# An attention block on one core: the third tile's maxima in two parts, the first tile's operands from their own halves, the transpose one matmul later, two slots reordered, rows of x fetched singly

## The chip, the cores and the metric

The kernel runs on one core of a Trainium2 chip. The metric is the device time of one execution in microseconds (us).

## What is computed

For each of 16 batches, x is 512 channels by 1024 positions, in float32:

```python
qkv = jnp.einsum('bchw,oc->bohw', x, w_qkv)           # 8 heads of 64
sim = jnp.einsum('bhdi,bhdj->bhij', q * SCALE, k)      # 1024 x 1024 a head
attn = jax.nn.softmax(sim, axis=-1)
out = jnp.einsum('bhij,bhdj->bhid', attn, v)
y = jnp.einsum('bchw,oc->bohw', out, w_out) + b_out
y = y * jax.lax.rsqrt(mean over channels of y*y + SCALE) * rms_scale
return y + x
```

## The kernel before, in words

The engines are TensorE (PE), VectorE (DVE), ScalarE (ACT) and GpSimd (POOL); SyncE (SP) issues the DMAs. Every engine runs an instruction list written out by hand for all batches, and semaphores join them. Precision comes from splits: an operand is kept as a rounded high part and the rest as a low part (`x_hi`, `x_lo`), and a projection does three matmuls for one.

**Slots and places.** A batch is 8 slots, a slot being one pair of heads with one half (512) of the queries. A slot has 16 places t = 0 to 15. At the even ones stand the scores of a step of 128 keys: for each of the two heads e, a matmul of `q_hl` (line 611) and one of `q_hm` (line 613) that adds in the low parts and subtracts the row maximum. At t = 1, 5, 9, 13 stand the values of the two steps before (line 626), at t = 1 also the sums of the slot before (line 549), and then the maxima of one tile of 128 queries for the next slot: M0 at t = 1 to M3 at t = 13. At t = 3 and 7 stands a projection of 12 matmuls of 512 columns (K, line 465) or 24 of 256 (V, line 498), at t = 11 the output projection O0 and O1 (line 524, 12 matmuls), at t = 15 the next queries' projection Q (line 465, 12 matmuls). Slots 0 and 1 also hold the mean of squares R at t = 7. Slot 5 has nothing at t = 3.

**Maxima.** A tile's maxima need the scores of its 128 queries with all 1024 keys for both heads: four matmuls into the four `aux` banks of PSUM, head 0 in banks 0 and 1, head 1 in banks 2 and 3. DVE reduces head 0 in two parts. Item M (line 894) takes bank 0 and one column of bank 1 and leaves its result in that column, which frees bank 0; item N (line 900) then reduces bank 1 into `maxima`. Head 1 is one reduction of two banks (line 890). Where the two matmuls of a pair go to different halves of the array's rows, they run side by side. Mostly the pair is the two key halves of one head (line 589), which needs q and k in both halves of the partitions: ACT repeats them (lines 702, 704 and 713), at the place in `REPEAT_Q_AT`. In the slots of `EARLY_MAXIMA` (1, 2, 7) the first tile pairs the two heads instead, each from its own half (line 571), and needs no repeated operand.

**Transpose.** After M3 has been reduced, T (line 509) turns `maxima` into rows with one matmul of 128 columns, and DVE multiplies them by a mask into `q_hm` (line 906, twice); then the next slot's scores may start. T stands inside Q, after its first six matmuls. It waits until DVE has consumed N30 and M31.

**Banks.** `claim` makes PE wait until a bank's last item is consumed. O0 takes banks 0 and 1; O1 takes bank 2 for its first three matmuls and bank 3 for the next three. K, V and Q take bank 0, T and R bank 2.

**DVE's list in a slot.** Per place: the items, then the reciprocals of the sums (`INVERT_SUMS_AT`, line 946, two halves), the normalising (line 953), the scaling of y (`SCALE_AT`, line 959; slots 1 and 2 only), x's low parts (`SPLIT_LOW_AT`, line 305; slots 5 and 6). ACT turns the normalised output into `o_hi` at t = 7 (line 759), ahead of the exponentials of t = 8 (line 695), and the next scores into the same PSUM bank wait for those. POOL adds up the probabilities (lines 1043 and 1047), makes `o_lo`, and in slots 1 and 2 scales rows of y (line 1065) and adds x (line 1078, `RESIDUAL_AT`).

Of the kernel before, what the change touches and what calls it, by code (L numbers as in the profile page):

```python
# [13 lines left out]
P = 128  # L14
# [12 lines left out]
INVERT_SUMS_AT = ((2, 5), (2, 5), (2, 5), (2, 2), (2, 5), (5, 5), (2, 2), (2, 2))  # L27
# [4 lines left out]
REPEAT_Q_AT = (0, 3, 3, 0, 0, 0, 0, 0)  # L32
# [3 lines left out]
EARLY_MAXIMA = (1, 2, 7)  # L36

# [12 lines left out]
SCALE_BY_ACT_AT = ((0, 3), (1, 3))  # L52
SCALE_AT = ({1: (1, 2), 2: (1, 3), 3: (1, 6)}, {2: (2, 2), 3: (2, 3)})
# [4 lines left out]
SPLIT_LOW_AT = ((5, 1), (5, 0), (5, 3), (5, 2), (6, 5), (6, 6), (6, 9), (6, 12))  # L58
SPLIT_BY_GPSIMD = (1, 3, 5, 7)


def items_at(slot, t, first, last):
# [4 lines left out]
    out = []  # L67
    if t % 4 == 1 and following:
        out.append((f"M{t // 4}0", 0))
        out.append((f"N{t // 4}0", 1))  # L70
        out.append((f"M{t // 4}1", 2))
    if t in (3, 7):
# [15 lines left out]
    if t == 15:  # L88
# [4 lines left out]
        if slot == 6 and projected:  # L93
# [5 lines left out]
             (7, "M10", 0), (7, "N10", 1), (7, "M11", 2), (7, "V2", 0), (7, "V3", 2), (7, "M20", 0), (7, "N20", 1), (7, "M21", 2),  # L99
# [21 lines left out]
def attention_kernel(nc, x, wqkv, wout, bias, scale, consts, out):  # L121
# [27 lines left out]
    with ctx:  # L149
# [91 lines left out]
        out_stored = sem("out_stored")  # L241
# [59 lines left out]
        def split_x(eng, c, n):  # L301
# [5 lines left out]
                              ).then_inc(x_split[c % 2], 1)  # L307
# [31 lines left out]
        def _(sp):  # L339
# [14 lines left out]
            for c in range(XS, 2 * KT):  # L354
                sp.wait_ge(x_split[c % 2], (c - XS) // 2 + 1)
                load_x(0, c)
# [21 lines left out]
            def finish_half(b, half, body_after=None):  # L378

                done = b * 2 + half  # L380
                cols = slice(half * HALF, (half + 1) * HALF)
                if half == 1 or body_after is None:
                    sp.wait_ge(out_stored, 16 * MT * done)
                for m in range(MT):
                    sp.dma_start(resid[:, m, :], x_v[b, m, :, cols]).then_inc(resid_loaded[m], 16)
                for m in range(MT):
                    sp.wait_ge(resid_added, 4 * done + m + 1)
                    sp.dma_start(out_v[b, m, :, cols], resid[:, m, :]).then_inc(out_stored, 16)

            def one(body):  # L390
# [5 lines left out]
                if not body.first:  # L396
                    finish_half(b - 1, 0, body)
                body.full(sp, 1, "Q")
                load_w(3)
                if not body.first:  # L400
                    finish_half(b - 1, 1, body)
                if not body.last:
# [8 lines left out]
                    if not body.first:  # L411

                        sp.wait_ge(out_stored, 16 * MT * 2 * b)
                    load_x(b + 1, XS - 1)
                    for c in range(XS, 2 * KT):
                        sp.wait_ge(x_split[c % 2], KT * (b + 1) + (c - XS) // 2 + 1)
# [5 lines left out]
            finish_half(B - 1, 0)  # L422
            finish_half(B - 1, 1)
            sp.wait_ge(out_stored, 16 * MT * 2 * B)
# [3 lines left out]
        def _(pe):  # L428
# [27 lines left out]
            def wait_x(body, half):  # L456

                for by in x_split:
                    pe.wait_ge(by, KT * (body.b + 1) + KT // 2 * (half + 1))

            def project(out_ap, w, cols, xcols, ks=range(KT)):

                for k in ks:
                    for n, (wp, xp) in enumerate(((0, x_hi), (1, x_hi), (0, x_lo))):
                        last = pe.matmul(out_ap, w[:, wp, k, cols], xp[:, k, xcols],  # L465
# [3 lines left out]
            def item(body, slot, name, ks=range(KT)):  # L469
                if name == "Q":  # L470
                    wait_w(body, (slot + SLOT_QUERIES) % SLOTS // 2, slot >= SLOTS - SLOT_QUERIES)
                    k = body.at(slot, name)[0] if ks[0] else claim(body, slot, name)
                    half = slot % 2
                    last = project(bank(k), w_ring[:, RING_OF[(slot + SLOT_QUERIES) % SLOTS // 2]], slice(0, P),
                                   slice(half * HALF, (half + 1) * HALF), ks)
                    if ks[-1] == KT - 1:
                        last.then_inc(aux_full[k], 1)
# [8 lines left out]
                elif name[0] == "V":  # L486
# [4 lines left out]
                    for i in range(2):  # L491
                        jt = 2 * int(name[1]) + i
                        n = 0
                        for c in range(KT):
                            if name == "V0" and slot == 5 and i == 0:
                                pe.wait_ge(x_split[c % 2], KT * (body.b + 1) + c // 2 + 1)
# [671 lines left out]
```

## Time and profile before

| | us |
|---|---|
| median of 3 runs | 4129.59 (4129.58 to 4131.71) |
| the profiled execution | 4120.75 |
| its span | 4119.0 |
| before the first scores | 56.1 |
| PE busy | 4022.6 |
| POOL busy | 2939.3 |
| DVE busy | 2885.2 |
| ACT busy | 2315.2 |

The span is from the first instruction of the program to the last. Matmuls are pipelined, so PE's busy share doesn't tell how well it is used; the distance from one matmul's start to the next one's does. A batch takes some 252 us, a slot 29.1 to 34.0.

### The profile page before, as it was taken

Reading aid. Unit: us, or ns where it says so; the run is one execution under the profiler, and the core shown is the slowest. Engines: PE = TensorE matmul, PEld = TensorE weight load, DVE = VectorE, ACT = ScalarE, POOL = GpSimd, SP = SyncE. Lnnn points to the kernel's source line nnn. Section 1 sums busy time; section 2 is a strip of 40 time slices with the busy share of each in tenths; the row PEclk is TensorE's granted clock in tenths of the full one; section 3 lists DMA queues with packets and bytes.
Section 4 is the critical chain, followed back from the end, with each engine's and each line's share of the span. In section 5 each row is a group of like instructions: output and inputs, shape, how many; then the busy total and the mean of one; then the engine's idle time right before and its main releaser. Section 6 shows DMA issues by size and latency. Waiting matters only on the chain.

```text
span 4119.0 us, 53911 instructions
## 1 busy us (share of the span) xinstructions
PE 4022.6 (98%) x18624; PEld 2413.1 (59%) x18624; DVE 2885.2 (70%) x3151; ACT 2315.2 (56%) x4044; POOL 2939.3 (71%) x2279
## 2 busy tenths in 40 slices
PE   7999999999999999999999999999999999999996
PEld 5555565665656555566655655556556565665652
DVE  5667776777766777676776766777667776777765
ACT  3556555565655656555565655655556565565653
POOL 4668676786776868767686776867768676686866
PEclk9999999999999999999999999999999999999998
DMA  3111111111111111112011110110111111111100
GB/s 144 41 37 57 52 42 62 52 52 41 63 51 42 52 42 67 47 42 72 32 62 52 37 67 31 62 52 37 67 52 42 52 44 62 49 52 42 65 19 31
DMA packets 71278, 212.25 MB, mean 52 GB/s; under 512 B 8152, under 2 KB 8280, under 8 KB 58208
## 3 DMA queue, kind: packets, MB, share of 16 engines
q1 hardware_dynamic: 71008, 208.80, 14.2%
q8 instruction: 151, 2.47, 0.3%
q14 instruction: 119, 0.97, 0.1%
HBM read 168.92 MB, written 39.85 MB: 51 GB/s over the span
## 4 chain that ended last, share of the span: by engine, by line
PE 77%; issue 7%; ACT 7%; DVE 5%; POOL 4%; DMA 0%; ACTq 0%; POOLq 0%; SPq 0%; DVEq 0%
PE pv L626 16%; PE aux L465 15%; PE score L611 11%; PE score L613 9%; PE aux L498 8%; PE aux L524 8%; PE aux L589 6%; ACT probs L695 3%; POOL prob_sum L1047 2%; ACT q_hm L704 1%; ACT q_hl L702 1%; DVE inv_sum L946 1%; ACT q_hl L720 1%; DVE maxima L890 1%; PE aux L509 1%
## 5 line engine op out<-in xcount | busy, mean ns | idle before, releaser
L1047 POOL TENSOR_TENSOR prob_sum<-prob_sum,probs 128x512 f32<-128x512 f32 x1536 | 1957.7, 1302 | 395.9 <-ACT probs L695 395.1
L695 ACT ACTIVATE probs<-score 128x512 f32<-128x512 f32 x2048 | 1110.5, 595 | 896.9 <-PE score L613 885.5
L626 PE MATMUL pv<-probs,v_sb 128*64 128x512 f32 x4096 | 993.3, 606 | 0.0
L894 DVE TENSOR_REDUCE aux<-aux 128x1 f32<-128x513 f32 x512 | 358.1, 699 | 904.8 <-PE aux L589 833.4
L611 PE MATMUL score<-q_hl,k_hh 128*128 128x512 f32 x2048 | 868.9, 424 | 13.7 <-ACT probs L695 11.9
L613 PE MATMUL score<-q_hm,k_l 72*128 72x512 f32 x2048 | 815.4, 398 | 0.0
L1043 POOL TENSOR_TENSOR prob_sum<-probs 128x512 f32<-128x512 f32 x256 | 352.4, 1398 | 461.4 <-ACT probs L695 461.4
L465 PE MATMUL aux<-x_hi,w_ring 128*128 128x512 f32 x2048 | 649.8, 398 | 15.6 <-DVE x_lo L305 11.1
L890 DVE TENSOR_REDUCE maxima<-aux 128x1 fp32r<-128x1024 f32 x512 | 621.4, 1214 | 0.0
L611 PEld LDWEIGHTS score<-q_hl,k_hh 128*128 128x128 f32 x2048 | 387.1, 189 | 278.8 <-issue 163.7
L626 PEld LDWEIGHTS pv<-probs,v_sb 128*64 128x64 f32 x4096 | 248.2, 136 | 483.0 <-issue 435.7
L946 DVE RECIPROCAL inv_sum<-inv_sum 128x256 f32<-128x256 f32 x256 | 438.7, 1735 | 9.5 <-ACT inv_sum L753 6.0
L465 PEld LDWEIGHTS aux<-x_hi,w_ring 128*128 128x128 f32 x2048 | 376.2, 190 | 101.1 <-issue 12.7
L613 PEld LDWEIGHTS score<-q_hm,k_l 72*128 72x128 f32 x2048 | 389.2, 190 | 59.3
L465 PE MATMUL aux<-x_lo,w_ring 128*128 128x512 f32 x1024 | 402.6, 393 | 0.0
L498 PE MATMUL aux<-w_ring,x_hi 128*128 128x256 f32 x2048 | 375.8, 284 | 1.7 <-DVE aux L894 1.7
L900 DVE TENSOR_REDUCE maxima<-aux 128x1 fp32r<-128x512 f32 x512 | 353.7, 691 | 17.6
L589 PEld LDWEIGHTS aux<-k_hh,q_hm 64*128 64x128 f32 x922 | 135.9, 185 | 391.2 <-issue 211.1
L589 PE MATMUL aux<-k_hh,q_hm 64*128 64x512 f32 x922 | 336.7, 445 | 10.5 <-DVE k_l L883 3.9
L589 PE MATMUL aux<-k_hh,q_hl 64*128 64x512 f32 x922 | 336.4, 444 | 0.0
L498 PEld LDWEIGHTS aux<-w_ring,x_hi 128*128 128x128 f32 x2048 | 326.3, 192 | 16.2 <-DVE aux L894 8.0
L498 PE MATMUL aux<-w_ring,x_lo 128*128 128x256 f32 x1024 | 290.6, 284 | 0.0
(84 smaller groups left out, 4898.6 us busy)
## 6 DMA issues: line engine op xcount, KB each, us to landing
w_ring<-w_split SPq DMA_DIRECT2D x93, 1024.0 KB, 4.8
x_stage<-x SPq DMA_DIRECT2D x128, 256.0 KB, 4.7
resid<-x SPq DMA_DIRECT2D x128, 256.0 KB, 5.8
out<-resid SPq DMA_DIRECT2D x128, 256.0 KB, 2.0
w_split<-w_ring SPq DMA_DIRECT2D x3, 1024.0 KB, 11.9
w_split<-y_sb SPq DMA_DIRECT2D x3, 1024.0 KB, 3.8
y_sb<-wqkv SPq DMA_DIRECT2D x4, 512.0 KB, 8.0
probs<-wqkv SPq DMA_DIRECT2D x2, 512.0 KB, 7.2
```

The source lines that it names most:

```text
L465: last = pe.matmul(out_ap, w[:, wp, k, cols], xp[:, k, xcols], start=(k == 0 and n == 0), stop=(k == KT - 1 and n == 2))
L498: last = pe.matmul(bank(k)[:, i * WCOLS:(i + 1) * WCOLS], xp[:, c, jt * P:(jt + 1) * P], w[:, wp, c, :], start=(n == 0), stop=(n == 3 * KT ...
L589: last = pe.matmul(bank(k + h), q_hi_at(nhalf, e, h, it), k_hh[rows, npair % 2, e, h * HALF:(h + 1) * HALF], start=True, stop=True)
L611: pe.matmul(score[e][:], k_hh[:, pair % 2, e, keys], q_hl[:, half, e, :], start=True, stop=False)
L613: pe.matmul(score[e][:], k_l1[0:D + 2 * IT, pair % 2, e, keys], q_hm[0:D + 2 * IT, half, e, :], start=False, stop=True).then_inc(score_rea ...
L626: pe.matmul(pv[half][e * D:(e + 1) * D, :], v_sb[:, pair // 2, j, (pair % 2) * P + e * D:(pair % 2) * P + (e + 1) * D], probs[:, j % 4, e, ...
L695: act.activation(probs[:, j % 4, e, :], score[e][:], ACT.Exp, scale=SOFT).then_inc(prob_ready, 1)
L890: dve.tensor_reduce(maxima[:, n:n + 1], bank(k, 2), AX_X, ALU.max).then_inc(aux_free[k], 1)
L894: dve.tensor_reduce(aux[:, first:first + 1], aux[:, k * HALF:first + 1], AX_X, ALU.max).then_inc(aux_free[k], 1)
L900: dve.tensor_reduce(maxima[:, n:n + 1], bank(k), AX_X, ALU.max).then_inc(aux_free[k], 1)
L946: dve.reciprocal(inv_sum[:, cols], inv_sum[:, cols]).then_inc(inv_ready, 1)
L1047: pool.tensor_tensor(prob_sum[:, e, :], prob_sum[:, e, :], probs[:, j % 4, e, :], ALU.add).then_inc(prob_added, 1)
```

## The change

The constants: slot 2 inverts its second half of the sums at t = 6 (before at 5), and scales rows 2 and 3 of y at t = 5 and 10 (before at 2 and 3). Slot 5 inverts at t = 2 and 5 (before both at 5), repeats the queries at t = 2 (before at 0), and DVE makes the low parts of pieces 0 and 1 of the next x at t = 0 (before pieces 0 and 2 at t = 1 and 3); POOL now has pieces 2, 3, 5, 7. ACT scales POOL's rows of y at t = 6 (before 3). The first tile's maxima use own halves in every slot. The third tile's head 1 is reduced in two parts like head 0. T follows Q's seventh matmul. The first score matmul of a slot goes ahead of the wait for the mask. SP has a semaphore for each of the four rows of the output; it loads a row of x for the second half as soon as that row of the first half is stored, and does so ahead of the weights of chunk 3.

```diff
-INVERT_SUMS_AT = ((2, 5), (2, 5), (2, 5), (2, 2), (2, 5), (5, 5), (2, 2), (2, 2))
+INVERT_SUMS_AT = ((2, 5), (2, 5), (2, 6), (2, 2), (2, 5), (2, 5), (2, 2), (2, 2))
-REPEAT_Q_AT = (0, 3, 3, 0, 0, 0, 0, 0)
+REPEAT_Q_AT = (0, 3, 3, 0, 0, 2, 0, 0)
-EARLY_MAXIMA = (1, 2, 7)
+SPLIT_SECOND = (2,)
+TURN_OF_MAXIMA = 7
-SCALE_BY_ACT_AT = ((0, 3), (1, 3))
-SCALE_AT = ({1: (1, 2), 2: (1, 3), 3: (1, 6)}, {2: (2, 2), 3: (2, 3)})
+SCALE_BY_ACT_AT = ((0, 6), (1, 6))
+SCALE_AT = ({1: (1, 2), 2: (1, 3), 3: (1, 6)}, {2: (2, 5), 3: (2, 10)})
-SPLIT_LOW_AT = ((5, 1), (5, 0), (5, 3), (5, 2), (6, 5), (6, 6), (6, 9), (6, 12))
-SPLIT_BY_GPSIMD = (1, 3, 5, 7)
+SPLIT_LOW_AT = ((5, 0), (5, 0), (5, 2), (5, 2), (6, 5), (6, 6), (6, 9), (6, 12))
+SPLIT_BY = ((0, 1, 4, 6), (2, 3, 5, 7))
...
-            def finish_half(b, half, body_after=None):
...
+            def load_resid(b, half):
                 for m in range(MT):
+                    if half == 1:
+                        sp.wait_ge(out_stored[m], 16 * (2 * b + 1))
+                    sp.dma_start(resid[:, m, :], x_v[b, m, :, half * HALF:(half + 1) * HALF]
+                                 ).then_inc(resid_loaded[m], 16)
...
+                    load_resid(b - 1, 0)
+                    store_half(b - 1, 0)
+                    load_resid(b - 1, 1)
                 body.full(sp, 1, "Q")
                 load_w(3)
...
+                        if turn and 3 * k + n == TURN_OF_MAXIMA:
+                            item(turn[0], turn[1], "T")
...
-                if it == 0 and slot in EARLY_MAXIMA or body.plan is pro:
+                if it == 0 or body.plan is pro:
+                    split = (True, it in SPLIT_SECOND)
...
-                if it == (1 if slot in EARLY_MAXIMA else 0):
+                if it == 1:
                     pe.wait_ge(q_repeated, 2 * (body.b * SLOTS + slot + 2))
...
+                    keys = slice(j * P, (j + 1) * P)
+                    pe.matmul(score[e][:], k_hh[:, pair % 2, e, keys], q_hl[:, half, e, :],
+                              start=True, stop=False)
                     if j == 0 and e == 0:
                         pe.wait_ge(mask_ready, body.b * SLOTS + slot + 1)
...
-                    keys = slice(j * P, (j + 1) * P)
-                    pe.matmul(score[e][:], k_hh[:, pair % 2, e, keys], q_hl[:, half, e, :],
-                              start=True, stop=False)
...
-                    if name[2] == "1":
+                    if name[2] == "1" and int(name[1]) not in SPLIT_SECOND:
```

## Rows read from the trace of the kernel before

**Rows 1.** The page: span, busy time by engine, TensorE's granted clock in 40 slices.
```profile
span 4119.0 us, 53911 instructions
...
PE 4022.6 (98%) x18624; PEld 2413.1 (59%) x18624; DVE 2885.2 (70%) x3151; ACT 2315.2 (56%) x4044; POOL 2939.3 (71%) x2279
...
PEclk9999999999999999999999999999999999999998
```

**Rows 2.** Waits: engine and line, released by; us in total, times, longest.
```profile
PEld aux L509 <- DVE maxima L890: 64.9, 128, 3.3
...
PEld aux L524 <- DVE maxima L890: 46.3, 111, 0.6
```

**Rows 3.** Groups of DVE by shape: count, busy us, mean ns, idle before.
```profile
L894 DVE TENSOR_REDUCE aux<-aux 128x1 f32<-128x513 f32 x512 | 358.1, 699 | 904.8 <-PE aux L589 833.4 <-PE aux L571 71.0
...
L900 DVE TENSOR_REDUCE maxima<-aux 128x1 fp32r<-128x512 f32 x512 | 353.7, 691 | 17.6
...
L959 DVE SCALAR_TENSOR_TENSOR y_sb<-y_sb,scale_sb,rms_a 128x512 f32<-128x512 f32 x83 | 100.8, 1235 | 1.2 <-ACT rms_a L793 0.7
```

**Rows 4.** Timeline, slot 0 of batch 4, M3 to the next scores.
```profile
1088.01 0.70 DVE L894 TENSOR_REDUCE aux<-aux 128x1 f32<-128x513 f32 x1 [0.45 <-PE aux L589]
...
1089.35 1.21 DVE L890 TENSOR_REDUCE maxima<-aux 128x1 fp32r<-128x1024 f32 x1
...
1090.02 0.19 PEld L465 LDWEIGHTS aux<-x_lo,w_ring 128*128 128x128 f32 x1
1090.24 0.40 PE L465 MATMUL aux<-x_lo,w_ring 128*128 128x512 f32 x1
...
1090.68 0.19 PEld L509 LDWEIGHTS aux<-neg_ident,maxima 128*128 128x128 f32 x1 [0.47 <-DVE maxima L890]
1090.71 0.30 PE L509 MATMUL aux<-neg_ident,maxima 128*128 128x128 f32 x1
...
1091.04 1.28 DVE L906 TENSOR_TENSOR q_hm<-aux,tile_mask 8x512 fp32r<-8x512 f32 x2 [0.48 <-PE aux L509]
...
1092.26 0.39 PE L611 MATMUL score<-q_hl,k_hh 128*128 128x512 f32 x1
```

**Rows 5.** Timeline, the same slot, M2 and the output projection.
```profile
1079.74 0.50 PE L589 MATMUL aux<-k_hh,q_hm 64*128 64x512 f32 x1
...
1081.72 1.21 DVE L890 TENSOR_REDUCE maxima<-aux 128x1 fp32r<-128x1024 f32 x1
...
1082.61 0.40 PE L524 MATMUL aux<-o_lo,wo_hi 128*128 128x512 f32 x1
...
1082.98 0.50 PE L524 MATMUL aux<-o_hi,wo_hi 128*128 128x512 f32 x1
...
1083.32 0.39 PE L524 MATMUL aux<-o_hi,wo_lo 128*128 128x512 f32 x1
```

**Rows 6.** Timeline, sums and M0: slot 0 (first two), slot 1.
```profile
1063.48 1.03 PE L549 MATMUL pv<-prob_sum,ones_d 128*64 128x512 f32 x4
...
1064.56 0.18 PEld L589 LDWEIGHTS aux<-k_hh,q_hm 64*128 64x128 f32 x1 [0.94 <-ACT q_hm L704]
...
1095.06 1.03 PE L549 MATMUL pv<-prob_sum,ones_d 128*64 128x512 f32 x4
...
1096.01 0.18 PEld L571 LDWEIGHTS aux<-k_hh,q_hm 64*128 64x128 f32 x1 [0.81 <-issue]
```

**Rows 7.** Timeline, slot 2 of batch 3 (starts at 872.42), M1 to the fifth scores.
```profile
883.11 1.60 DVE L959 SCALAR_TENSOR_TENSOR y_sb<-y_sb,scale_sb,rms_a 128x512 f32<-128x512 f32 x1
...
884.18 0.50 PE L611 MATMUL score<-q_hl,k_hh 128*128 128x512 f32 x1
...
888.39 0.39 PE L611 MATMUL score<-q_hl,k_hh 128*128 128x512 f32 x1
```

**Rows 8.** Timeline, slot 5 of batch 3 (starts at 966.35), reciprocals to the sixth scores.
```profile
978.56 3.35 DVE L946 RECIPROCAL inv_sum<-inv_sum 128x256 f32<-128x256 f32 x2
...
983.84 0.50 PE L611 MATMUL score<-q_hl,k_hh 128*128 128x512 f32 x1 [0.24 <-ACT probs L695]
```

More of the change, by code:

```diff
@@ L71, in items_at @@
         out.append((f"M{t // 4}1", 2))
+        if t // 4 in SPLIT_SECOND:
+            out.append((f"N{t // 4}1", 3))
     if t in (3, 7):
@@ L240, in attention_kernel @@
         resid_loaded = [sem(f"resid_loaded{i}") for i in range(MT)]
-        out_stored = sem("out_stored")
+        out_stored = [sem(f"out_stored{i}") for i in range(MT)]
         x_loaded = [sem(f"x_loaded{i}") for i in range(XS)]
@@ L421, in _ @@
             run_bodies(sp, one)
-            finish_half(B - 1, 0)
-            finish_half(B - 1, 1)
-            sp.wait_ge(out_stored, 16 * MT * 2 * B)
+            wait_stored(2 * (B - 1))
+            for half in range(2):
+                load_resid(B - 1, half)
+                store_half(B - 1, half)
+            wait_stored(2 * B)
         @block.tensor
@@ L456, in wait_x, with project @@
             def wait_x(body, half):
[L458 to L463, printed above, removed]
+                for c in (max(c for c in by if c < KT * (half + 1)) for by in SPLIT_BY):
+                    wait_piece(pe, c, body.b + 1)
+            def project(out_ap, w, cols, xcols, turn=None):
+                for k in range(KT):
                     for n, (wp, xp) in enumerate(((0, x_hi), (1, x_hi), (0, x_lo))):
+                        if turn and 3 * k + n == TURN_OF_MAXIMA:
+                            item(turn[0], turn[1], "T")
                         last = pe.matmul(out_ap, w[:, wp, k, cols], xp[:, k, xcols],
@@ L467, in project, with item @@
                 return last
-            def item(body, slot, name, ks=range(KT)):
+            def item(body, slot, name, turn=None):
                 if name == "Q":
                     wait_w(body, (slot + SLOT_QUERIES) % SLOTS // 2, slot >= SLOTS - SLOT_QUERIES)
-                    k = body.at(slot, name)[0] if ks[0] else claim(body, slot, name)
+                    k = claim(body, slot, name)
                     half = slot % 2
[L474 to L477, printed above, removed]
+                    project(bank(k), w_ring[:, RING_OF[(slot + SLOT_QUERIES) % SLOTS // 2]], slice(0, P),
+                            slice(half * HALF, (half + 1) * HALF), turn).then_inc(aux_full[k], 1)
                 elif name[0] == "K":
@@ L563, in maxima_of_tile @@
                 npair, nhalf = divmod(nslot, 2)
-                if it == 0 and slot in EARLY_MAXIMA or body.plan is pro:
-                    ks = [claim(body, slot, f"M{it}0"), claim(body, slot, f"M{it}1", two=True)]
-                    claim(body, slot, f"N{it}0")
+                if it == 0 or body.plan is pro:
+                    split = (True, it in SPLIT_SECOND)
+                    ks = [claim(body, slot, f"M{it}{e}", two=not split[e]) for e in range(2)]
+                    for e in range(2):
+                        if split[e]:
+                            claim(body, slot, f"N{it}{e}")
                     for h in range(2):
@@ L583, in maxima_of_tile @@
                 for e in range(2):
-                    k = claim(body, slot, f"M{it}{e}", two=e == 1)
+                    split = e == 0 or it in SPLIT_SECOND
+                    k = claim(body, slot, f"M{it}{e}", two=not split)
                     for h in range(2):
-                        if h == 1 and e == 0:
-                            claim(body, slot, f"N{it}0")
+                        if h == 1 and split:
+                            claim(body, slot, f"N{it}{e}")
                         rows = slice(h * D, (h + 1) * D)
@@ L653, in one @@
                         elif "Q" in names:
[L654 to L656 removed]
+                            item(body, slot, "Q", (body, slot))
                             for name in names:
@@ L990, in one @@
                         if (slot, t) in SPLIT_LOW_AT and not body.last:
-                            if SPLIT_LOW_AT.index((slot, t)) not in SPLIT_BY_GPSIMD:
-                                split_x(dve, SPLIT_LOW_AT.index((slot, t)), body.b + 1)
+                            for c in SPLIT_BY[0]:
+                                if (slot, t) == SPLIT_LOW_AT[c]:
+                                    split_x(dve, c, body.b + 1)
             dve.memset(ones_d[:], 1.0).then_inc(const_set, 1)
@@ L999, in _ @@
             split_w(0, 0)
-            for c in range(0, 2 * KT, 2):
+            for c in SPLIT_BY[0]:
                 split_x(dve, c, 0)
-                if c == 2:
+                if c == 1:
                     split_w(1, VA)
@@ L1101, in one @@
                             split_squares_low(2 * (body.b - 1) + slot)
-            for c in range(1, 2 * KT, 2):
+            for c in SPLIT_BY[1]:
                 split_x(pool, c, 0)
```

48 lines of the change are left out of this document (24 added, 24 removed).

## The prediction

> **What bounds the kernel now.** I read the page first: PE is busy nearly the whole span, its granted clock at the full level (2.4 GHz) after the prologue, and no other engine is busy above 71% [rows 1]. So time is gained only where the step from one matmul's start to the next is longer than it need be. The usual step for 512 columns is 0.23 us. Next the waits, for those of PE that come back in every slot: the transpose T waits for DVE's last maximum 128 times, the second output projection 111 times [rows 2]. Then the timeline around each, for what the wait costs PE; and last the starts of all score matmuls (line 611), sixteen a slot, which show in which slots a step between scores is longer than in others with the same work. The reader is to see that all losses are short, on PE, and repeat in each batch.
>
> **T one matmul later.** Q's sixth matmul starts at 1090.24. DVE's reduction ends at 1089.35 + 1.21 = 1090.56, T's weights load at 1090.68 and T runs at 1090.71 [rows 4]: 0.47 after the sixth matmul, where 0.23 is usual. The loss is 0.23 to 0.24, in all slots alike (the mean step over the 128 T is 0.468). After the change the seventh matmul fills it: it starts at 1090.47, T's turn is at 1090.70, and DVE allows it at 1090.71. One matmul fits as exactly as the trace can tell. Gain 0.233 in each slot that has Q beside T: 8 in each of 15 batches and 6 in the last, 126 x 0.233 = 29.4 us. What this uncovers is the mask: T now has 5 matmuls behind it, so the scores start 1.33 after T and not 1.55 (1092.26 - 1090.71). DVE's first mask multiply ends 0.33 + 0.64 = about 1.0 after T (half of the 1.28) and the second at 1.61 [rows 4]. With the first score matmul ahead of the wait, what needs the masks starts at 1.56 (head 0) and 2.03 (head 1), its weights 0.23 before. With the 0.12 that T's load took after DVE's end both are in time, the second by under 0.1. Without this reorder the second would be late by 0.1 to 0.2; I count the reorder itself at nothing.
>
> The Trainium skill ("TensorE: Matmul & The Clock Gate", The mechanism) says that a weight load overlaps matmuls in flight only when its row group differs. By that T's own load of 0.19 would be exposed wherever T stands, and the move would gain about 0.05 a slot. The trace disagrees: the 128-row load at 1090.02 runs inside the matmuls of 128 rows before it [rows 4].
>
> **Third tile in two parts.** M2 starts at 1079.74; head 1's reduction runs from 1081.72 to 1082.93. Output matmul 6 starts at 1082.61, matmul 7, which needs bank 2, at 1082.98 and matmul 8 at 1083.32: steps of 0.37 and 0.34 for 0.23 each [rows 5], a loss of 0.25. In two parts bank 2 comes free after 0.70 [rows 3], at 1082.42, before its turn; bank 3 after another 0.03 + 0.69, at 1083.14, and is needed by a load at 1083.3. Gain 0.25 x 111 = 27.8 us. The 111 are the waits [rows 2]; in slot 5 PE comes late for another reason and doesn't wait. The cost is on DVE: 0.70 + 0.03 + 0.69 for 1.21, 0.21 a slot, 27 us in all. It lies in DVE's idle time: before M3's first reduction DVE has been idle for 0.45 in slot 0 [rows 4], the least of all slots by the same view, of which about 0.15 goes because PE reaches M3 sooner. If the cover were gone, M3's reductions and with them T would be late by as much as is lacking.
>
> **First tile from own halves.** In slot 0 M0 starts 1.08 after the sums, when ACT's repeat of q ends; in slot 1, which has the form already, 0.95 [rows 6]. Gain 0.125 in slots 0, 3, 4, 5, 6, so 80 x 0.125 = 10.0 us. Head 0's banks are then full 0.2 later, which slots 1, 2 and 7 bear without loss. M1 waits for the repeats instead, and they end 4 us earlier.
>
> **Slot 2.** DVE's scaling of row 3 (1.60 us) ends only at 884.71, so M1's reductions come late and K1, which needs bank 0, too: the fourth scores start at 884.18, the fifth at 888.39, 4.21 after, where slot 0 without R has 3.80 [rows 7]. Over the 15 batches that scale y this step is 4.13 to 4.21 eight times, 4.44 six times, 6.05 once; the step before is 3.56 to 4.47. Together these lose 13.5 us. After the change nothing stands before M1 but half a reciprocal, but behind it come the scaling of row 2, the other reciprocal (1.74), the normalising (0.69) and then K1's two subtractions (1.38), and M2 needs K1's bank. From M1's start: reductions done at 3.2, scaling 4.4, reciprocal 6.1, normalised 6.8, K1's bank free 8.2; M2's turn comes at 3.56 + 3.80 = 7.36. It waits 0.86, 12.9 us over 15 batches. Net gain 0.6. The scaling is the uncertain term: it took 1.60 here with POOL at work and 1.24 on the mean [rows 3, 7], with 0.65 and 1.81 as its ends by the same view. I take the mean, since POOL adds probabilities without a pause at that point and DVE would come in the middle of one addition. The ends give slot 2 a net of +9 and -8 us. The Trainium skill ("SBUF — State Buffer", Who interferes with whom) says that a DVE instruction with two SBUF inputs and a reading GpSimd instruction exclude each other for a whole instruction, whoever is first. The two durations of one form agree.
>
> Row 3's scaling moves to t = 10, and POOL waits for it inside its step 4, with three steps of additions queued behind. I put its sum of x and row 3 at 25.6 from the slot's start. ACT's copy of O1's last row waits for that; the exponentials behind it end at 26.9, and the eighth scores need them at 27.3. POOL's last addition ends some 1.1 before the sums need it. Nothing, with 0.4 to spare.
>
> **Slot 5.** The normalising waits for two reciprocals in a row (3.35), ACT holds the exponentials behind `o_hi`, and the sixth scores start only at 983.84 [rows 8], 3.87 after the fifth for 3.56: 0.31. One half moves to t = 2, and the low parts of x to t = 0, where DVE waits for M0 anyway (two at 0.65 with POOL idle, done at 4.5, M0's reductions at 4.58). Also 0.06 where ACT's repeat leaves the second exponentials free. 0.37 x 15, and 1.8 in the last batch, where slot 5 has no V: 7.4 us. If the two low parts took 1.8 each, M0's reductions would be late by 2.3, and M1's banks with them: 2 us a batch, 30 in all.
>
> **The rest at nothing.** ACT's two scalings at t = 6 lie in its idle time, and leave slot 1's repeat of q earlier, at most 0.08 a batch, 1 us in all. The single fetches and the four semaphores act on SP; the loads ahead of chunk 3's weights wait for stores that land some 5 us before the end of slot 1, and those weights are first needed two slots later. What is queued behind SP's waits has that room. POOL's and DVE's pieces of x in the prologue: within 0.3 us either way.
>
> **Sum.** 29.4 + 27.8 + 10.0 + 0.6 + 7.4 = 75.2 us. The profiled execution took 4120.75 and becomes 4045.5; the median of the runs is 8.8 above it, and becomes 4054.4. A difference of 0.2%, 8 us, is about what a measurement of this kernel can tell from none.
>
> **The rivals.**
>
> T's pause stays, as a cost of its own (an exposed load, or DVE just late again): 29.4 x 0.8 less, 4078. For it: the fit has no margin. Against: T's load started 0.12 after the reduction's end in 127 of 128, so it waited. Chance 0.08.
>
> DVE becomes the wait: its extra 0.21 a slot reaches PE at O1's second bank or at M3. 4054 + 111 x 0.2 = 4077 if in full. For: margins of 0.15 and 0.3. Chance 0.12.
>
> Slot 2 or 5 worse than counted: the long ends, 8 + 15 or so, 4077. Chance 0.12.
>
> Slot 2 without its new wait (the scaling finds POOL's gap): 4054 - 9 = 4045. Chance 0.08.
>
> Slower: in slot 2 POOL, held at row 3, finishes the additions late; PE's sums, and ACT's exponentials of the reused probability buffers, wait for them. It decides from (75 + 8) / 15 = 5.5 us a batch. By my schedule POOL has 1.1 to spare and is idle twice before, so it would have to be wrong by 6.6: 4140. Chance 0.03.
>
> **How the numbers follow.** The forecast, 4054, has 0.57 with its own range of 4046 to 4064. The cases near 4077 have 0.32 in all, the one at 4045 0.08, the slower one 0.03. The range 4039 to 4083 leaves out less than 0.2. Faster by over 0.2% 0.94, within 0.2% 0.03, slower 0.03.
>
> **What would show it.** T's step 0.24 in place of 0.47 and no idle time of the weight load before it; output matmuls 7 and 8 at 0.23; M0 0.95 after the sums in all slots; one new wait, of M2 in slot 2 for line 883, near 0.9; slot 5 at 28.4 us from 29.1. The prediction is wrong if T's weights still wait over 0.2 for DVE, if line 509 or 524 keeps its wait, or if POOL's list becomes continuous through slots 2 and 3.

## The result, and the profile after

The changed kernel takes 4029.51 us (median of 4, 4027.74 to 4029.71), the kernel before 4129.59 (4 runs, 4121.6 to 4131.71). The ratio is 0.976, 95% interval 0.9743 to 0.9777: faster by 2.4%. The forecast was 4054 with a range of 4039 to 4083, so the sign was right and the gain was too small, outside the range. The profiled execution took 4027.74 (4120.75 before), its span fell by 93.0.

The page of the changed kernel (beside [rows 1]):

```profile
span 4026.0 us, 53767 instructions
...
PE 3951.3 (98%) x18624; PEld 2427.4 (60%) x18624; DVE 2890.0 (72%) x3279; ACT 2320.3 (58%) x4044; POOL 2919.8 (73%) x2279
...
PEclk9999999999999999999999999999999999999997
...
L916 DVE TENSOR_REDUCE aux<-aux 128x1 f32<-128x513 f32 x640 | 446.7, 698 | 849.7 <-PE aux L611 636.3
```

PE is as full as before and does the same matmuls in 71 us less busy time. DVE has 128 reductions more, PE 208 and SP 32 waits more that are instructions of their own, and yet the program has 144 instructions fewer: 512 waits of DVE are gone. They are what the prediction missed, as experiment 9 shows.

Its waits, beside [rows 2] (line 527 is T, 611 the maxima of M1 to M3, 903 DVE's subtraction for K):

```profile
PEld aux L527 <- DVE maxima L910: 26.8, 128, 3.2
...
PE aux L611 <- DVE k_l L903: 10.0, 15, 0.7
```

T's wait fell from 64.9 to 26.8, 0.21 on the mean, and did not go away. The 46.3 of the output projection have no row any more. The new wait is M2's in slot 2, 15 times, as forecast.

The timeline at the end of slot 0 of batch 4, beside [rows 4]: M3, DVE's reductions, Q's seventh matmul, T, the masks, the next scores.

```profile
1062.91 0.50 PE L611 MATMUL aux<-k_hh,q_hm 64*128 64x512 f32 x1
...
1063.48 0.70 DVE L916 TENSOR_REDUCE aux<-aux 128x1 f32<-128x513 f32 x1 [0.38 <-PE aux L611]
...
1064.82 1.21 DVE L910 TENSOR_REDUCE maxima<-aux 128x1 fp32r<-128x1024 f32 x1
...
1066.01 0.40 PE L485 MATMUL aux<-x_hi,w_ring 128*128 128x512 f32 x1
1066.15 0.19 PEld L527 LDWEIGHTS aux<-neg_ident,maxima 128*128 128x128 f32 x1 [0.17 <-DVE maxima L910]
1066.25 0.23 PE L527 MATMUL aux<-neg_ident,maxima 128*128 128x128 f32 x1
1066.31 0.45 PE L485 MATMUL aux<-x_hi,w_ring 128*128 128x512 f32 x1
...
1066.51 1.28 DVE L928 TENSOR_TENSOR q_hm<-aux,tile_mask 8x512 fp32r<-8x512 f32 x2 [0.48 <-PE aux L527]
...
1067.52 0.40 PE L626 MATMUL score<-q_hl,k_hh 128*128 128x512 f32 x1
```

T stands 0.24 after the matmul ahead of it, as forecast. But two more things changed. DVE starts 0.57 after M3's first matmul, where it was 0.64 (M3 of before started at 1087.37, the reduction at 1088.01 [rows 4]). And the matmul behind T follows it by 0.06, where it was 0.13.

The same slot, third tile and output projection, beside [rows 5]: head 1's two reductions and matmuls 6 to 8.

```profile
1057.44 0.69 DVE L916 TENSOR_REDUCE aux<-aux 128x1 f32<-128x513 f32 x1
...
1058.16 0.69 DVE L922 TENSOR_REDUCE maxima<-aux 128x1 fp32r<-128x512 f32 x1
...
1058.40 0.39 PE L542 MATMUL aux<-o_lo,wo_hi 128*128 128x512 f32 x1
...
1058.63 0.40 PE L542 MATMUL aux<-o_hi,wo_hi 128*128 128x512 f32 x1
...
1058.87 0.39 PE L542 MATMUL aux<-o_hi,wo_lo 128*128 128x512 f32 x1
```

Bank 2 is free at 1058.13, 0.5 ahead of its turn; all steps are 0.23 to 0.24.

Sums and M0 in slot 0, beside [rows 6]:

```profile
1039.38 1.03 PE L567 MATMUL pv<-prob_sum,ones_d 128*64 128x512 f32 x4
...
1040.34 0.18 PEld L592 LDWEIGHTS aux<-k_hh,q_hm 64*128 64x128 f32 x1 [0.81 <-issue]
```

0.96 after the sums for 1.08, with no releaser on ACT. Slot 2 of batch 3 (starts at 852.09), beside [rows 7]:

```profile
866.33 1.23 DVE L981 SCALAR_TENSOR_TENSOR y_sb<-y_sb,scale_sb,rms_a 128x512 f32<-128x512 f32 x1
867.48 1.74 DVE L968 RECIPROCAL inv_sum<-inv_sum 128x256 f32<-128x256 f32 x1
867.67 0.39 PE L626 MATMUL score<-q_hl,k_hh 128*128 128x512 f32 x1
...
869.86 1.38 DVE L903 TENSOR_TENSOR k_l<-aux,k_hh 64x512 fp32r<-64x512 f32 x2
...
871.29 0.49 PE L611 MATMUL aux<-k_hh,q_hm 64*128 64x512 f32 x1 [0.65 <-DVE k_l L903]
...
871.95 0.50 PE L626 MATMUL score<-q_hl,k_hh 128*128 128x512 f32 x1
```

The scaling takes 1.23 (I had taken 1.24). M2 waits for K1's bank, and the sixth scores come 4.28 after the fifth for 3.56. The two steps ahead of that are at 3.56 and 3.82 to 3.84 in all 15 batches that scale y. Slot 5 of batch 3, beside [rows 8], fifth and sixth scores:

```profile
957.79 0.40 PE L626 MATMUL score<-q_hl,k_hh 128*128 128x512 f32 x1
...
961.35 0.51 PE L626 MATMUL score<-q_hl,k_hh 128*128 128x512 f32 x1
```

3.56 for 3.87, and no wait for ACT. The starts of all score matmuls in the two traces, step by step, give the sum, in us:

| | forecast | measured |
|---|---|---|
| T and Q (last step of a slot) | 29.4 | 38.7 |
| output projection | 27.8 | 31.0 |
| first tile | 10.0 | 9.9 |
| slot 2, net | 0.6 | 2.0 |
| slot 5 | 7.4 | 7.3 |
| slot 1 | up to 1 | 1.0 |
| start of the program and first slot | 0 | 3.9 |
| rest | 0 | -0.8 |
| span | 75.2 | 93.0 |

So the profiled execution is 17.8 faster than forecast (4045.5), 9.3 of it in T's term. Another 7.0 come from the step to the median: I carried over the 8.8 by which the profiled execution of before lies under its median; after the change it is 1.8.

### The profile page after: what moved, and what is told of

It reads as the page before. It is cut to its first block, busy times and chain, and to the rows that moved or that the text cites. A ratio compares the mean times of both kernels' runs of the same rounds, so it can differ in the third digit from the quotient of the medians.

```text
span 4026.0 us, 53767 instructions
## 1 busy us (share of the span) xinstructions
PE 3951.3 (98%) x18624; PEld 2427.4 (60%) x18624; DVE 2890.0 (72%) x3279; ACT 2320.3 (58%) x4044; POOL 2919.8 (73%) x2279
## 4 chain that ended last, share of the span: by engine, by line
PE 94%; DVE 3%; issue 2%; POOL 1%; ACT 0%; DMA 0%; POOLq 0%; SPq 0%; ACTq 0%; DVEq 0%
PE pv L648 23%; PE aux L485 17%; PE score L626 14%; PE score L635 11%; PE aux L516 9%; PE aux L542 9%; PE aux L611 6%; PE pv L567 3%; PE aux L592 2%; DVE inv_sum L968 1%; DVE maxima L910 1%; DVE k_l L903 1%; DVE y_sb L981 0%; DVE aux L916 0%; ACT probs L715 0%
## 5 line engine op out<-in xcount | busy, mean ns | idle before, releaser
L916 DVE TENSOR_REDUCE aux<-aux 128x1 f32<-128x513 f32 x640 | 446.7, 698 | 849.7 <-PE aux L611 636.3
L1066 POOL TENSOR_TENSOR prob_sum<-probs 128x512 f32<-128x512 f32 x256 | 338.3, 1343 | 505.9 <-ACT probs L715 505.9
L910 DVE TENSOR_REDUCE maxima<-aux 128x1 fp32r<-128x1024 f32 x384 | 465.9, 1213 | 0.0
L922 DVE TENSOR_REDUCE maxima<-aux 128x1 fp32r<-128x512 f32 x640 | 442.4, 691 | 22.0
L485 PEld LDWEIGHTS aux<-x_hi,w_ring 128*128 128x128 f32 x2048 | 386.8, 189 | 95.6 <-issue 12.4
L516 PEld LDWEIGHTS aux<-w_ring,x_hi 128*128 128x128 f32 x2048 | 328.4, 192 | 13.9 <-DVE aux L916 2.4
L611 PEld LDWEIGHTS aux<-k_hh,q_hm 64*128 64x128 f32 x762 | 112.1, 184 | 320.2 <-issue 244.2
L611 PE MATMUL aux<-k_hh,q_hm 64*128 64x512 f32 x762 | 278.0, 444 | 10.0 <-DVE k_l L903 10.0
L611 PE MATMUL aux<-k_hh,q_hl 64*128 64x512 f32 x762 | 277.7, 444 | 0.0
```

The source lines that it names most:

```text
L516: last = pe.matmul(bank(k)[:, i * WCOLS:(i + 1) * WCOLS], xp[:, c, jt * P:(jt + 1) * P], w[:, wp, c, :], start=(n == 0), stop=(n == 3 * KT ...
L611: last = pe.matmul(bank(k + h), q_hi_at(nhalf, e, h, it), k_hh[rows, npair % 2, e, h * HALF:(h + 1) * HALF], start=True, stop=True)
L910: dve.tensor_reduce(maxima[:, n:n + 1], bank(k, 2), AX_X, ALU.max).then_inc(aux_free[k], 1)
L916: dve.tensor_reduce(aux[:, first:first + 1], aux[:, k * HALF:first + 1], AX_X, ALU.max).then_inc(aux_free[k], 1)
L922: dve.tensor_reduce(maxima[:, n:n + 1], bank(k), AX_X, ALU.max).then_inc(aux_free[k], 1)
```

## The experiments

Kernels are changed from the changed kernel unless it says otherwise. "Over" and "under" are differences of medians against 4029.51. The kernel before, timed beside each group again, had medians of 4123.7 (0 to 3), 4127.19 (4 to 7), 4127.62 (9 to 12) and 4128.01 (13, 14). The numbers go from 7 to 9. The changed kernel itself was timed only in the four runs above, and the kernel before moves by up to 6 us from group to group (4129.59 in the first). A difference of a few microseconds therefore rests on the steps in the traces, which are given beside it. Experiments 13 and 14 ran on a second chip; the kernel before took the same there within 0.4 us.

**0. The kernel before again**, unchanged.

> The kernel before, unchanged, timed again. The four timed runs of it lie at 4121.6 and near 4130, those of the changed kernel within 2 us. Theory A (slot 2's race for SBUF between VectorE and GpSimd comes out otherwise from run to run): times scatter by up to 10 us and slot 2's steps before the fourth and fifth scores lose between 10 and 25 us in all, 13.5 in the first profile. Theory B (the spread was of the chip that day): times within 2 us of each other, slot 2 loses 13 to 14.

4124.54 (11 runs, 4117.73 to 4127.64) beside 4123.7 (15 runs, 4118.07 to 4129.03); ratio 1.0002 (0.9993 to 1.001). These 11 executions spread over 10 us, those of the changed kernel over 2, but the latter are four, all at a mean granted clock of 0.993, where these have 0.991 to 0.993. Slot 2's two steps lose as much in this trace as in the first one, within 1 us, though in other batches. So the traces do not show that the race between VectorE and GpSimd (Theory A) makes the scatter.

**1. T after six matmuls.**

```diff
-TURN_OF_MAXIMA = 7
+TURN_OF_MAXIMA = 6
```

> The changed kernel with the transpose back behind the sixth matmul. Prediction's size (the wait for VectorE alone, 0.233 a slot): 29 us slower, 4059. Theory now (the wait also costs the weight load behind the transpose, 0.07, since it can't be fetched ahead): 0.30 a slot, 38 us slower, 4068. Rival (the extra 0.07 comes from the score matmul ahead of the mask wait): 29 us slower, and the step from the transpose to the next matmul stays 0.066.

4057.62, 28.1 over; ratio 0.9842 (0.9829 to 0.9855). The end of slot 0 of batch 4:

```profile
1075.00 0.40 PE L485 MATMUL aux<-x_lo,w_ring 128*128 128x512 f32 x1
1075.37 0.19 PEld L527 LDWEIGHTS aux<-neg_ident,maxima 128*128 128x128 f32 x1 [0.40 <-DVE maxima L910]
1075.40 0.30 PE L527 MATMUL aux<-neg_ident,maxima 128*128 128x128 f32 x1
1075.53 0.68 PE L485 MATMUL aux<-x_hi,w_ring 128*128 128x512 f32 x2
```

With T in its old turn the two steps around it are 0.40 and 0.13. They were 0.47 and 0.13 before, and are 0.24 and 0.06 in the changed kernel. The turn is worth 0.23 a slot, as forecast; the 38 us of "Theory now" were wrong, and so was the rival's step of 0.066, which is 0.13. The turn does not explain the drop from 0.47 to 0.40: something else brings DVE 0.07 forward in every slot.

**2. Third tile whole.**

```diff
-SPLIT_SECOND = (2,)
+SPLIT_SECOND = ()
```

In the prologue, item N21 goes too.

> The changed kernel with head 1 of the third tile reduced in one instruction of two banks. Prediction: 28 us slower, 4057. From the trace after: 0.25 to 0.30 in seven slots and slot 5 too, now that nothing else holds it back there: 31 to 35 us slower, 4061 to 4064. Rival (VectorE's 27 us less work gives something back): less than 25 us slower.

4056.59, 27.1 over; ratio 0.984 (0.9826 to 0.9853). The step of the output projection is 0.18 to 0.24 longer in every slot. The prediction's 28 was right, my 31 to 35 from the trace after was not.

**3. First tile from repeated operands** in slots 0, 3, 4 and 6.

```diff
+EARLY_MAXIMA = (1, 2, 5, 7)
...
-                if it == 0 or body.plan is pro:
+                if it == 0 and slot in EARLY_MAXIMA or body.plan is pro:
...
-                if it == 1:
+                if it == (1 if slot in EARLY_MAXIMA else 0):
```

> The changed kernel with slots 0, 3, 4 and 6 pairing the key halves again for the first tile and waiting for the repeated queries. Prediction: 0.125 in 4 slots of 16 batches, 8 us slower, 4037.5. Rival (the repeats are no longer late since the scalar engine starts sooner): no difference.

4039.09, 9.6 over; ratio 0.9797 (0.9782 to 0.9812). By the steps it is 0.125 in each of the four slots, 8 us in all; the profiled execution's first scores also came 2.7 later.

**4. Slot 2 in the old order.**

```diff
-INVERT_SUMS_AT = (..., (2, 6), ...)
+INVERT_SUMS_AT = (..., (2, 5), ...)
-SCALE_AT = (..., {2: (2, 5), 3: (2, 10)})
+SCALE_AT = (..., {2: (2, 2), 3: (2, 3)})
```

> The changed kernel with slot 2's reciprocal and two scalings at their old places. Prediction: 0.6 us slower. Theory now: the old order loses 13.5 us or more in 15 batches and varies from run to run, the new one 11.0 and doesn't: 3 to 12 us slower, 4033 to 4041, with a scatter over 3 us. Rival (the gain over the median came from elsewhere): within 2 us, no scatter.

4022.69, 6.8 *under* the changed kernel; ratio 0.9748 (0.9734 to 0.9761). In batches 1 to 14 (of 0 to 15) the steps are 6.2 us shorter. M2's wait is gone, and the third and fourth steps between scores (to the fourth and fifth scores) are 3.56 and 4.06 to 4.15 in all 15 batches, where the kernel before, with the same order, has 3.56 to 4.47 and 4.13 to 6.05. So the old order's erratic loss vanished without its being reordered, and the new order is a loss.

**5. The mask's wait first**, ahead of the first score matmul.

```diff
-                    keys = slice(j * P, (j + 1) * P)
-                    pe.matmul(score[e][:], k_hh[:, pair % 2, e, keys], q_hl[:, half, e, :],
-                              start=True, stop=False)
                     if j == 0 and e == 0:
                         pe.wait_ge(mask_ready, body.b * SLOTS + slot + 1)
...
                     elif j == 0:
                         body.consumed(pe, slot - 1, "T")
+                    keys = slice(j * P, (j + 1) * P)
+                    pe.matmul(score[e][:], k_hh[:, pair % 2, e, keys], q_hl[:, half, e, :],
+                              start=True, stop=False)
```

> The changed kernel with the wait for the mask back ahead of the first score matmul. Prediction: the second mask is late by 0.1 to 0.2 a slot less the slack of 0.2 that a weight load has, so 0 to 13 us slower, 4030 to 4043. Rival (the reorder is worth its own matmul, 0.23 a slot): 29 us slower, 4059.

4033.1, 3.6 over; ratio 0.9771 (0.9757 to 0.9784). The first step of a slot is 0.02 longer, 2.2 us in batches 1 to 14. I had put the lateness that the reorder covers at 0.1 to 0.2. The edit also gives PE 254 more waits that are instructions of their own (54021 instructions for 53767), so it stays open whether the 0.02 is a late mask or these.

**6. Slot 5 as before.**

```diff
-INVERT_SUMS_AT = (..., (2, 5), (2, 2), (2, 2))
-REPEAT_Q_AT = (0, 3, 3, 0, 0, 2, 0, 0)
-SPLIT_LOW_AT = ((5, 0), (5, 0), (5, 2), (5, 2), ...)
-SPLIT_BY = ((0, 1, 4, 6), (2, 3, 5, 7))
+INVERT_SUMS_AT = (..., (5, 5), (2, 2), (2, 2))
+REPEAT_Q_AT = (0, 3, 3, 0, 0, 0, 0, 0)
+SPLIT_LOW_AT = ((5, 1), (5, 0), (5, 3), (5, 2), ...)
+SPLIT_BY = ((0, 2, 4, 6), (1, 3, 5, 7))
...
-                if c == 1:
+                if c == 2:
                     split_w(1, VA)
```

> The changed kernel with slot 5's list (reciprocals, repeat of the queries, pieces of x and who makes their low parts) as before, in the prologue too. Prediction: 7.4 us slower. If the 2.2 us that the first scores came earlier are of the order of the pieces of x, 9.6 us slower, 4039, and the first scores at 56.1. Rival (the 2.2 us are of the third tile's split or of chance): 7.4 us slower, first scores at 54.

4040.27, 10.8 over; ratio 0.9788 (0.9775 to 0.9801). Slot 5 is 0.46 longer (0.18 in its second step, 0.31 in its fifth, 0.03 less in its sixth), the last batch 4.4 longer, the first scores 1.8 later. That last part is no proof for the order of the pieces of x: the two traces of the kernel before, with one and the same order, have their first scores at 56.1 and 53.5.

**7. T after eight matmuls.** `TURN_OF_MAXIMA = 8`.

> The changed kernel with the transpose one matmul later still. Theory (seven matmuls fill the wait exactly): nothing to gain, and the masks come later by one matmul: the second is late by 0.1 to 0.2, so 0 to 20 us slower. Rival (a wait is left behind seven, 26.8 us of idle weight loads): up to 8 us faster.

4027.06, 2.4 under; ratio 0.9756 (0.9743 to 0.9769). The last step is 3.944 for 3.954, and all steps of batches 1 to 14 together are 2.3 us shorter: T's turn had almost no more to give, and nothing was lost by later masks.

**9. The second wait put back.** The missed edit is in DVE's part: before, a two-part reduction waited for its own bank *and* for the next one; after, for the next one alone, since the later matmul implies the earlier.

```diff
                     else:
+                        k = body.full(dve, slot, name)
                         body.full(dve, slot, "N" + name[1:])
-                        k, _ = body.at(slot, name)
```

> The changed kernel with VectorE's list for a tile's first reduction as before: a wait for the bank of the first part and then one for the second, where the change has only the latter. Theory (the second wait costs an instruction of its own, 0.067 between the maxima's matmuls and their first reduction, and this reaches the transpose in every slot): 0.067 x 126 = 8.4 us slower, 4038. Rival (the 0.067 came from the first tile's form or the fetches): no difference.

4039.22, 9.7 over; ratio 0.9787 (0.9774 to 0.9801). Its page's first line, and the end of slot 0 of batch 4:

```profile
span 4038.1 us, 54407 instructions
```

```profile
1069.17 0.50 PE L611 MATMUL aux<-k_hh,q_hm 64*128 64x512 f32 x1
...
1069.81 0.70 DVE L916 TENSOR_REDUCE aux<-aux 128x1 f32<-128x513 f32 x1 [0.45 <-PE aux L611]
...
1072.27 0.40 PE L485 MATMUL aux<-x_hi,w_ring 128*128 128x512 f32 x1
1072.48 0.19 PEld L527 LDWEIGHTS aux<-neg_ident,maxima 128*128 128x128 f32 x1 [0.24 <-DVE maxima L910]
1072.51 0.30 PE L527 MATMUL aux<-neg_ident,maxima 128*128 128x128 f32 x1
1072.64 0.45 PE L485 MATMUL aux<-x_hi,w_ring 128*128 128x512 f32 x1
```

640 instructions more than the changed kernel, one for each of DVE's 640 two-part reductions (x640 on the page). The instructions by source line show what they are in the kernel before, where there were 512:

```profile
L288 DVEq EVENT_SEMAPHORE  x512: 21/21/21, 25.5 to 4045.8; - x171
```

A second wait is an instruction of its own on DVE's queue. It takes 0.021, and with it the reduction starts 0.64 after M3's first matmul and not 0.57. In the kernel before, that instruction stands at 1087.94, 0.57 after M3's first matmul, which is when the reduction itself starts in the changed kernel; the reduction follows 0.04 after its end. T's step is 0.24 and the one behind it 0.13: these are the steps that I had costed. The step behind T falls to 0.06 only when DVE is early enough for T's weights to load ahead of T's turn, which takes the turn and the one wait together.

**10 and 14. The kernel before with one wait**, the same edit alone, twice.

```diff
-                    k = body.full(dve, slot, name)
+                    k, _ = body.at(slot, name)
                     if name[2] == "1":
+                        body.full(dve, slot, name)
```

> The kernel before with this one wait taken out of VectorE's list and nothing else. Theory: the transpose comes 0.067 earlier in every slot (8.4 us), and in slot 2 VectorE's scaling is ready 0.067 earlier and goes ahead of GpSimd's addition every time, which takes away some 8 of slot 2's 13.5 us: 12 to 17 us faster than before, near 4110. Rival (no race, only the wait): 8 us faster.

> The kernel before with DVE's second wait taken away, run a second time. Its first median was 30.7 below the kernel before (4096.95), its profiled span only 18.5 below. If the profiled execution was simply an outlier (its last batch 3.1 longer, prologue 1.4 longer), the median is again 4095 to 4099 and this profile's span is near 4096 to 4101, 20 us less over batches 1 to 14. If the first median was the chance, it is 4100 to 4108 now.

4096.95 and 4097.05 beside 4127.62 and 4128.01: ratios 0.9927 (0.9913 to 0.994) and 0.9924 (0.9911 to 0.9936), 31 us by one wait, where I had expected 12 to 17. In batches 1 to 14 both traces show some 22 us less: 0.07 in every last step (8.5), 0.07 in the step of the output projection (7), and 6 to 7 us in two steps of slot 2, far more than 0.07 a batch. Both profiled executions were the longest of their five (4102.25 and 4100.06) and that of before was short (4120.75), so the profiles show less than the medians. The medians of executions with the same recorded clock, within a group, lie 29 to 32 apart, so the clock doesn't explain the rest.

What happened in slot 2 is the scaling of row 2 by DVE. In the 19 batches of the two traces in which GpSimd was not held up by a late row of x, it took 0.65 every time.

**11. The rows of x behind the weights** (on top of 4): the four loads of the second half after chunk 3's weights and after all four stores, as before the change.

```diff
                     store_half(b - 1, 0)
-                    load_resid(b - 1, 1)
                 body.full(sp, 1, "Q")
                 load_w(3)
                 if not body.first:
+                    wait_stored(2 * b - 1)
+                    load_resid(b - 1, 1)
```

> The changed kernel with slot 2's list as before, and the second half's rows of x loaded behind chunk 3's weights and after all four stores, as before. Theory (the single fetches matter where slot 2 scales early: in 5 of 15 batches of the kernel before, GpSimd's first sum of x waited for its row): 1 to 4 us slower than with the early loads, 4024 to 4027, with rows late in some batches. Rival (the loads are hidden either way): 4022.7, no row late.

4020.79, 1.9 under experiment 4; ratio 0.9742 (0.9729 to 0.9756). GpSimd's first sum of x starts at 6.17 from slot 2's start in all batches of experiment 4, at 6.29 to 6.66 in four of these, and slot 2's third and fourth steps lose 1.5 us more in 14 batches, in the range that I had expected, but the median does not show it. The single fetches bring nothing that the times show.

**12. Best version**: experiment 4, T after eight, and only row 3's scaling at its new place.

```diff
-TURN_OF_MAXIMA = 7
+TURN_OF_MAXIMA = 8
-INVERT_SUMS_AT = (..., (2, 6), ...)
+INVERT_SUMS_AT = (..., (2, 5), ...)
-SCALE_AT = (..., {2: (2, 5), 3: (2, 10)})
+SCALE_AT = (..., {2: (2, 2), 3: (2, 10)})
```

> The changed kernel with the reciprocals of slot 2 as before, row 2's scaling at place 2 as before, row 3's at place 10 as changed, and the transpose after eight matmuls. From slot 2 as before 4022.7; less 2 for the transpose; less 0.27 x 15 = 4 if K1 no longer waits: 4017. Rival (GpSimd, held at row 3, is late for the sums): slower than 4022.

4015.62 (4012.12 to 4016.4), 13.9 under; ratio 0.9728 (0.9715 to 0.9742). Slot 2's third to sixth steps are 3.56, 3.83, 3.56 and 3.82: no wait is left in them.

**13. Two waits in the old slot 2**: experiment 4 with the edit of 9.

> The changed kernel with slot 2 in its old order and early fetches of x (measured at 4022.7), with the second wait put back ahead of DVE's two-part reductions. It tells what the second wait does in slot 2. If the two waits only delay each reduction by 0.067, the cost is that of the same edit in the changed kernel, 9.7: 4032, slot 2's fourth and fifth steps stay at 3.56 and 4.1 in all batches, and DVE's scaling of row 2 takes 0.65 there. If the delay makes DVE lose the race with GpSimd for that scaling (it won by 0.03 with one wait), the scaling takes 1.5 to 1.8, slot 2 loses another 0.4 to 0.9 a batch, 6 to 13 us, the time is 4038 to 4046 and scatters by some 5 to 10 us from run to run, and POOL's first sum of x waits for its row in some batches.

4053.6 (4046.89 to 4054.82); ratio 0.9819 (0.9805 to 0.9832). That is 30.9 over experiment 4, the same 31 as in 10 and 14, and more than the race theory had expected. Slot 2 of batch 4, in experiment 4 (starts at 1097.55) and then here (starts at 1102.53): DVE's scalings of rows 2 and 3 (line 981), GpSimd's addition beside the first, M1's reduction.

```profile
1106.20 0.65 DVE L981 SCALAR_TENSOR_TENSOR y_sb<-y_sb,scale_sb,rms_a 128x512 f32<-128x512 f32 x1
1106.22 3.01 POOL L1066 TENSOR_TENSOR prob_sum<-probs 128x512 f32<-128x512 f32 x2
...
1108.19 1.59 DVE L981 SCALAR_TENSOR_TENSOR y_sb<-y_sb,scale_sb,rms_a 128x512 f32<-128x512 f32 x1
...
1109.81 0.70 DVE L916 TENSOR_REDUCE aux<-aux 128x1 f32<-128x513 f32 x1
```

```profile
1111.20 2.95 POOL L1066 TENSOR_TENSOR prob_sum<-probs 128x512 f32<-128x512 f32 x2
1111.25 1.77 DVE L981 SCALAR_TENSOR_TENSOR y_sb<-y_sb,scale_sb,rms_a 128x512 f32<-128x512 f32 x1
...
1114.36 1.58 DVE L981 SCALAR_TENSOR_TENSOR y_sb<-y_sb,scale_sb,rms_a 128x512 f32<-128x512 f32 x1
1114.47 0.46 PE L611 MATMUL aux<-k_hh,q_hm 64*128 64x512 f32 x1 [0.80 <-DVE k_l L903]
...
1115.97 0.70 DVE L916 TENSOR_REDUCE aux<-aux 128x1 f32<-128x513 f32 x1
```

With one wait DVE comes at 8.65 from the slot's start, GpSimd at 8.67: DVE's scaling takes 0.65 in all 15 batches and GpSimd is held. With two, DVE comes at 8.72, GpSimd at 8.68, and in 13 of 15 batches DVE is held until GpSimd is through: 1.77 to 1.79. M1 then waits for K's bank and its reduction is 1.2 later. Slot 2 loses 16.0 us in 14 batches by this, the last steps 7.8 by the 0.07, of 24.8 by the spans. The profiled execution here had the highest clock of the five (0.994, the others 0.992 and 0.993) and lies 6.7 under their median; in experiment 4 it lies 0.6 under. So the spans show less than the medians. The kernel before is the same race, undecided. In batch 4 it was lost:

```profile
1132.71 2.97 POOL L1043 TENSOR_TENSOR prob_sum<-probs 128x512 f32<-128x512 f32 x2
1132.75 1.81 DVE L959 SCALAR_TENSOR_TENSOR y_sb<-y_sb,scale_sb,rms_a 128x512 f32<-128x512 f32 x1
```

In eight of its 15 batches it took 0.65, with DVE at the same 8.71 to 8.72; in three it took 1.78 to 1.81, and in four 1.17 to 1.53, those where GpSimd's first sum of x had waited for its row (6.82 to 7.18 for 6.18). Over all traces with the old place of this scaling, and counting only batches with no late row: with one wait DVE won 60 of 60 (experiments 4, 10, 11, 12, 14), with two it won 14 and lost 20 of 34 (13 and both traces of the kernel before).

## Why the prediction was right in kind and too small

The forecast was 24.9 us too long. Of these 9.3 are in T's term, 7.0 in the step from the profiled execution to the median, 3.9 in the start of the program, 3.2 in the output projection, 1.4 in slot 2; the rest cancels.

**T one matmul later: mechanism right, size off (29.4, measured 38.7).** This is the term of the sum that was mis-sized. The step in it was "DVE's reduction ends at 1089.35 + 1.21 = 1090.56 ... One matmul fits as exactly as the trace can tell": it took DVE's start over from the trace of before, while the diff removes one of DVE's two waits ahead of it. The two steps around T are together 0.60 before and 0.30 after, by the median over all 128. Experiment 1 gives 0.23 of that to the turn, experiment 9 0.07 to the wait: 0.07 x 126 = 8.8, and 9.7 by the times. The prediction's sum has no term for this wait: it put it at nothing without a reason. With the wait put back the kernel takes 4039.2, at the lower end of the stated range. (The mean step of 0.468 in the prediction leaves out two T's of 3.31 and 1.86; with all 128 it is 0.50. The medians used here do not depend on them.)

One of the prediction's own signs of being wrong came: T's weights still wait for DVE, 26.8 us over 128, 0.21 on the mean. But T's step is down to 0.24, so what is left is a wait of the load alone, under Q's seventh matmul.

The load of T's weights (0.19, at 1066.15) begins 0.14 after Q's seventh matmul of 128 rows and under it, and T follows that one by 0.24: the load costs nothing. The Trainium skill ("TensorE: Matmul & The Clock Gate", The mechanism) lets a load overlap only when the row group differs; the trace disagrees again.

**Third tile: 27.8, measured 31.0.** Here the loss was counted by waits, 111 of them; by the steps it is 0.28 for each and not 0.25. Undoing it costs 27.1. With one wait the unsplit tile loses less (0.18 to 0.24; experiment 2), because the wait is worth 0.07 there too (experiments 10 and 14).

**First tile: 10.0, measured 9.9; slot 5: 7.4, measured 7.3.** Both by their working. The low parts of x take 0.65 each in slot 5, as assumed.

**Slot 2: 0.6, measured 2.0, for the wrong alternative.** Each piece came true: the scaling at 1.23, M2's wait at 0.71 to 0.76 a batch (11.0; forecast 0.86 and 12.9). But I compared with the 13.5 that the old order lost in the profile. With the second wait gone it would lose 4 (experiment 4), so in the changed kernel the reorder is a loss of 7. The prediction took the 0.65 and 1.81 of one form as "ends" and did not ask what picks between them. It is 0.07 of DVE's start. The Trainium skill ("SBUF — State Buffer", Who interferes with whom) says that the first to issue keeps the port for its whole instruction. That one of the two is held for the whole of the other agrees: 0.65 against 1.77, and GpSimd's own 1.73 to 1.83 against 1.27 to 1.29. That the first one wins is borne out only where DVE is recorded first; the kernel before won and lost with the same recorded starts, GpSimd's ahead.

**The start: nothing, measured 3.9, and it is chance.** The first scores come at 51.9 to 57.7 us over the 16 profiled executions of all kernels, 53.95 in the changed one, 56.12 and 53.48 in the two of the one before. The changed kernel gains nothing by itself there that these traces could show. TensorE's granted clock from 55 to 100 us is 0.94 after and 0.89 before, both with stretches at the lower of its two levels (1.2 GHz); from 100 to 3980 us it is full in both.

**Median over profile: 8.8, measured 1.8.** It was no constant, and this is 7.0 of the miss. Why the kernel before scatters more stays open. Part of any kernel's scatter goes with the clock: experiment 4 took 4022.13 to 4023.04 in four executions at 0.993 and 4026.25 in one at 0.992. Within one group of runs and at one recorded clock, the kernel before spread over up to 7.6 (three at 0.991) and 5.7 (five at 0.992), the changed kernel over 2.0 (four) and its variants over at most 2.6, but the clock is recorded to 0.001, which is 4 us of the span. That the race makes the difference is argued and not shown: the two traces of the kernel before lose the same in slot 2, and experiment 13, in which the race is nearly always lost, spreads over 2.6 at 0.993 (two executions), 7.9 over all its clocks. For the same reason it stays open where the some 10 us lie by which the medians of 10 and 14 fell more than the profiles show.

**The rivals.** T's pause did not stay: 0.24 in place of 0.47. DVE did not become the wait: its 0.21 a slot lie in idle time; 0.38 of it is left before M3's first reduction in slot 0. Slot 2's wait came, and slot 5 was not worse. GpSimd was not late: no kernel was slower. The rival "slot 2 without its new wait" (4045) has its price in experiment 4, 6.8 for my 9, but not its way: the wait goes with the old order once DVE wins the race. All of them, the range too, assumed that the diff had been costed in full.

## What to carry to other kernels

Cost every line of a diff that adds or removes a wait, even one that looks like a rearrangement: a second wait on a DVE instruction was 0.07 us each time here, and 10 to 31 us in all. Where two engines meet at one resource within some hundredths of a microsecond, treat the outcome as undecided, look at both durations of the form, and order the work so that a small shift cannot turn it; an edit measured before such a race is settled is credited or blamed for it. An execution's distance from its median is scatter, and not to be added to a forecast.

## What the runs showed of the hardware that was not expected

- A second wait on DVE is an EVENT_SEMAPHORE of 0.021 on its queue, and delays the waiting reduction by 0.07 (0.64 after the matmul for 0.57).
- The matmul behind a 128-column one follows it by 0.06 when that one's weights were loaded ahead of its turn, by 0.13 when they were waited for.
- DVE's start of 8.65 or 8.72 against GpSimd's 8.67 decides between 0.65 and 1.78 for one scaling. At 8.71 to 8.73, with GpSimd recorded at 8.66 to 8.70, it went either way (14 won, 20 lost); at 8.63 to 8.66, recorded ahead of GpSimd by up to 0.06, DVE won 60 of 60. Where GpSimd is recorded first, by 0.02 to 0.06, the recorded order does not tell who has the port.
